# Slot attentions: one ring of six PSUM banks, four heads of turned scores at once, and the softmax maximum in two halves

## The chip, the cores and the metric

The kernel runs on one core of one Trainium2 chip. The metric is device time in microseconds (us) for one execution of the whole program. The program is a 16-layer hybrid network, so a time is a sum over layers that run one after another with a barrier between them.

## What is computed

The input is x of 8 sequences with 256 tokens each and width 128. The layers around the change are multi-head attentions with 16 heads of 8 dimensions. Cut to what matters, each of them computes, for a sequence:

```
q, k, v = h @ Wq (+ bq), h @ Wk (+ bk), h @ Wv (+ bv)      # 16 heads of 8
s = q @ k.T * scale                                        # 256 x 256 a head; causal or windowed in two layers
p = softmax(s)
o = p @ v
```

`L0_attn_b` is causal, `L2_attn_b` has no mask, `L3_attn_b` has a causal window of 64, and the encoder layer `L3_ffn` (it comes twice, as layers 13 and 15) runs, for each of the 8 sequences, the two experts that a gate picked; each is an unmasked attention, a layer norm, a two-layer network of 512 hidden units and another layer norm. All of it is float32.

## The kernel before

Four kinds of stage share the code of the change: three calls of `slot_attention_stage` (8 units, one for each sequence) and two of `encoder_stage` (16 units, sequence times expert). A unit is cut into `NC` = 4 chunks of `HP` = 4 heads, and each head sits in a slot of 32 partitions. One step of the stage's loop (`for u in a.steps`) works on a chunk. So a slot attention has 32 chunk steps and an encoder 64.

A chunk's work runs over several engines:

- **scores** (`slot_scores_pe`, L628): TensorE multiplies queries with keys, four heads in four row strips of the array at once, into `S`, four PSUM banks, one a head. Masked stages add the mask by eight more products (L647). VectorE takes the negative row maximum from `S` (`slot_max_dve`, L756).
- **turned maximum** (`slot_turn_max_pe`, L688): TensorE turns the maxima into `X`, the one bank that all side work shares; VectorE adds them to the queries (`slot_add_max_dve`, L771) and so makes `qA`.
- **turned scores** (`slot_turned_scores_pe`, L652): keys times `qA`, that is the score already less its maximum, with keys on the partitions. Two heads at a time, p = 0 and p = 1, into `E`, two banks. ScalarE takes the exponential of each pair of heads into `sT` (`slot_exp_act`, L725).
- **PV** (`slot_pv_pe`, L670): the exponentials times v into `OB`; ScalarE copies (`slot_out_act`, L732), TensorE turns the copy (`slot_turn_out_pe`, L698), and VectorE divides by the sum (`slot_norm_dve`, L779).

There is no scheduler: each engine executes its instructions in the order in which its block writes them, and waits at semaphores. Between the chunk's operations stand the **items**: projections of q and k (`qk`) and of v (`v`), the turn of the normed input (`h`), and for the encoder the turn of the attention's output (`t`), its projection (`y`), the turn of the first norm's output (`t1`), and the two-layer network (`f1`, `f2`, `f3`). Each step has at most one early and one late item, from the tables at the head of the stage. In the encoder every step has both: early `qk`, `f1`, `y`, `f3`, late `t1`, `t`, `f2`, `v` for the chunks 0 to 3. A slot attention has `qk` and `v` early in chunks 0 and 1 and `h` late in chunk 3; the windowed one also has `y` early in 3 and `t` late in 2.

Every item is a product into bank `X`, then a copy out of it: by VectorE for `y` and `f3`, by ScalarE for all others. The bank is handed on in the fixed order early item, late item, turned maximum. TensorE waits before each (`slot_x_pe`) until the one before it has been copied out:

```
n = a.number[item]
if n:
    pe.wait_ge(b.sems.x_used, n)
```

Of the kernel before, what the change touches and what calls it, by code (L numbers as in the profile page):

```python
# [384 lines left out]
class SlotPlan:  # L385
# [34 lines left out]
    def at(self, kt):  # L420

        return slice(kt * self.n[0], kt * self.n[0] + self.n[kt])

# [86 lines left out]
class SlotBuffers:  # L510


    def __init__(self, st, a):
# [5 lines left out]
        self.sT = st.sb("sT", [P, 2, a.HP, TT * a.n[0]])  # L519
# [4 lines left out]
        self.S = st.ps("S", [P, a.HP, 512])  # L524
        self.E = st.ps("E", [P, 2, 512])
# [102 lines left out]
def slot_scores_pe(pe, g, a, b, u):  # L628
# [4 lines left out]
    if u:  # L633
        pe.wait_ge(s.maxed, u)
    for t in range(TT):
        lo, hi = a.keys[t]
        for h in range(a.HP):
            rows = slice(32 * h, 32 * (h + 1))
            last = pe.matmul(b.S[:, h, t * T:t * T + hi - lo], b.qk[rows, r % 2, 0, c, t * P:(t + 1) * P],  # L639
                             b.qk[rows, r % 2, 1, c, lo:hi], start=(t == 0), stop=(a.mask is None and t == TT - 1),  # L640
                             skip_group_check=True, tile_position=(32 * h, 0))
    if a.mask is not None:
        for h in range(a.HP):
            for t in range(TT):
                lo, hi = a.masked[t]
                at = t * T + lo - a.keys[t][0]
                last = pe.matmul(b.S[:, h, at:at + hi - lo], g.ident_bf[:], g.masks[a.mask][:, t, lo:hi],  # L647
                                 start=False, stop=(t == TT - 1), skip_group_check=True)
    last.then_inc(s.scored, 1)


def slot_turned_scores_pe(pe, a, b, u, p):  # L652
# [3 lines left out]
    if p == 0:  # L656
        pe.wait_ge(s.x_used, a.number[("m", u)] + 1)
    if 2 * u + p:
        pe.wait_ge(s.expd, 2 * u + p)
    for kt in range(TT):  # L660
        lo, hi = a.queries[kt]
        for i in range(2):
            rows = slice(32 * (2 * p + i), 32 * (2 * p + i + 1))
            last = pe.matmul(b.E[:, i, a.at(kt)], b.qk[rows, r % 2, 1, c, kt * P:(kt + 1) * P],  # L664
                             b.qA[rows, u % 2, lo:hi], start=True, stop=True, skip_group_check=True,
                             tile_position=(32 * (2 * p + i), 0))
    last.then_inc(s.st_mm, 1)


def slot_pv_pe(pe, a, b, j):  # L670
# [8 lines left out]
    for kt in range(TT):  # L679
        lo, hi = a.queries[kt]  # L680
        for h in range(a.HP):
            last = pe.matmul(b.OB[32 * h:32 * (h + 1), lo:hi], b.v[:, r % 2, kt, a.HP * c + h, :],  # L682
                             b.sT[:, j % 2, h, a.at(kt)], start=(kt == 0), stop=(kt == TT - 1),
# [4 lines left out]
def slot_turn_max_pe(pe, g, a, b, u):  # L688
# [3 lines left out]
    pe.wait_ge(s.maxed, u + 1)  # L692
# [32 lines left out]
def slot_exp_act(act, a, b, u, p):  # L725
# [3 lines left out]
    act.activation(b.sT[:, u % 2, 2 * p:2 * p + 2, 0:a.width], b.E[:, :, 0:a.width], ACT.Exp).then_inc(s.expd, 1)  # L729
# [8 lines left out]
def slot_cut_pool(pool, a, b, u):  # L738

    s = b.sems  # L740
    for p in range(2):
        pool.wait_ge(s.expd, 2 * u + p + 1)
        m = b.sT[:, u % 2, 2 * p:2 * p + 2, :].rearrange("p h (k q) -> p (h k) q", k=TT)
# [12 lines left out]
def slot_max_dve(dve, a, b, u):  # L756

    s = b.sems
    dve.wait_ge(s.scored, u + 1)
    if a.mask is None:  # L760
        ins = dve.tensor_reduce(b.negm[:, u % 2, :, a.HD::32].rearrange("p t h -> p h t"),  # L761
                                b.S[:].rearrange("p h (t k) -> p h t k", t=TT), AX_X, ALU.max, negate=True)
    else:
        for t in range(TT):
            lo, hi = a.keys[t]
            ins = dve.tensor_reduce(b.negm[:, u % 2, t, a.HD::32], b.S[:, :, t * T:t * T + hi - lo], AX_X, ALU.max,  # L766
# [26 lines left out]
def slot_attention_stage(nc, g, name, W, scale, mask=None, project=False):  # L793
# [7 lines left out]
    with Stage(nc, name) as st:  # L801
# [9 lines left out]
        with nc.Block() as block:  # L811
# [6 lines left out]
            def _(pool):  # L818
# [3 lines left out]
                for u in range(U + 1):  # L822
# [4 lines left out]
                    if not project and (r := a.ends(u - 1)) is not None:  # L827
                        xb = g.x[:, TT * r:TT * r + TT, :]
                        pool.wait_ge(s.o_norm, u)
# [5 lines left out]
            def _(pe):  # L835
# [14 lines left out]
                for u in a.steps:  # L850
                    if u + 1 < U:
                        slot_scores_pe(pe, g, a, b, u + 1)
                    for item in a.early(u):
                        other(item)
                    if 0 <= u < U:
                        slot_turned_scores_pe(pe, a, b, u, 0)
                    for item in a.late(u):
                        other(item)
                    if 0 <= u - 1 < U:
                        slot_pv_pe(pe, a, b, u - 1)  # L860
                    if 0 <= u < U:
                        slot_turned_scores_pe(pe, a, b, u, 1)
# [2481 lines left out]
```

## Time and profile before

| | us |
|---|---|
| median of 3 runs | 3464.14 |
| lowest and highest run | 3460.72 to 3464.31 |
| the profiled execution's own time | 3461.5 |
| its span | 3459.8 |
| scores of the causal attention, first to last | 698.4 to 857.0 |
| of the unmasked attention | 1638.7 to 1812.9 |
| of the first encoder | 2332.7 to 2746.3 |
| of the windowed attention | 2801.4 to 2953.6 |
| of the second encoder | 2996.3 to 3411.9 |

The profile shows for each instruction when it started and how long it took; where an engine was idle before it, it names what released it. A float32 product of the code appears in the profile as two matmuls, so the eight products of scores appear as x16. A chunk step is read from one start of the scores (L639) to the next, and a unit is four such steps. PE is TensorE's matmuls, PEld its weight loads, ACT ScalarE, DVE VectorE, POOL GpSimd. PEclk is the granted TensorE clock: 1.00 is 2.4 GHz, 0.50 is 1.2 GHz.

### The profile page before, as it was taken

The page shows a single profiled execution, that of the slowest core. Times are in us where ns is not written, and L with a number is a line of the kernel's source. Part 1 is how long each engine was busy: PE and PEld are TensorE (multiplying, and loading weights), DVE is VectorE, ACT ScalarE, POOL GpSimd, SP SyncE. Part 2 cuts the span into 40 slices and gives each one's busy share as a digit, 9 for nine tenths or more (in the row PEclk, how much of TensorE's full clock was granted, in tenths as well). Part 3 has the DMA queues.
Part 4 walks back from the last instruction along what each step waited for, and adds up shares of the span by engine and source line. Part 5 has one row for each costly group of instructions (what it writes and reads, how often), then busy time and mean ns, then how long its engine had stood idle before and what let it go on. Part 6 is the DMA issues. An engine that isn't in the chain of part 4 may idle for free. (4 is left out here: it accounts for less than half of the span.)

```text
span 3459.8 us, 60788 instructions
## 1 busy us (share of the span) xinstructions
PE 3006.9 (87%) x23920; PEld 2002.9 (58%) x23920; DVE 1991.5 (58%) x4069; ACT 1409.0 (41%) x2886; POOL 959.6 (28%) x1321
## 2 busy tenths in 40 slices
PE   5689699999699879776996699979999979799997
PEld 1234377766477646455665466756666657466665
DVE  5998655445655568642563466655556545455564
ACT  4344244434344324212452244434554434245543
POOL 1455333223223110122003433330222245212222
PEclk7799799999799969777897799988999989699998
DMA  1000100010000000010100000002222101112221
GB/s 75 1 1 0 50 1 1 1 29 20 1 1 1 1 1 2 1 65 19 27 20 21 7 1 1 1 7 62 67 65 70 50 21 27 51 38 67 65 70 42
DMA packets 46937, 90.94 MB, mean 26 GB/s; under 512 B 6052, under 2 KB 34524, under 8 KB 45888
## 3 DMA queue, kind: packets, MB, share of 16 engines
q1 hardware_dynamic: 44608, 86.43, 8.2%
q8 instruction: 194, 3.18, 0.4%
q0 software_dynamic: 2048, 0.61, 0.1%
q14 instruction: 87, 0.71, 0.1%
HBM read 70.16 MB, written 19.14 MB: 26 GB/s over the span
## 5 line engine op out<-in xcount | busy, mean ns | idle before, releaser
L729 ACT ACTIVATE s_sT<-s_E 128x1024 f32<-128x1024 f32 (+2 forms) x448 | 424.6, 948 | 487.0 <-PE s_E L664 486.2
L664 PE MATMUL s_E<-s_qA,s_qk 32*128 32x256 f32 (+2 forms) x3584 | 484.3, 388 | 15.1 <-ACT s_sT L729 6.1
L664 PEld LDWEIGHTS s_E<-s_qA,s_qk 32*128 32x128 f32 x3584 | 313.0, 189 | 164.8 <-ACT s_sT L729 76.4
L761 DVE TENSOR_REDUCE s_negm<-s_S 128x8 f32<-128x2048 f32 x160 | 366.9, 2293 | 69.8 <-PE s_S L639 61.6
L776 DVE TENSOR_TENSOR s_qA<-s_qk,s_X 128x256 f32<-128x256 f32 x224 | 94.4, 421 | 415.3 <-PE s_X L694 415.3
L639 PE MATMUL s_S<-s_qk 32*128 32x256 f32 (+2 forms) x3584 | 255.9, 402 | 15.1 <-DMA s_qk<-s_pk 15.1
L682 PE MATMUL s_OB<-s_sT,s_v 128*32 128x256 f32 (+2 forms) x3584 | 227.7, 372 | 4.9 <-POOL s_sT L751 1.9
L2470 POOL TENSOR_TENSOR all_hT<-s0s_hs,s0s_cb 128x1024 f32<-128x1024 f32 x64 | 150.5, 2352 | 197.0 <-DVE s0s_hs L2504 179.8
L639 PEld LDWEIGHTS s_S<-s_qk 32*128 32x128 f32 x3584 | 158.8, 195 | 59.9 <-issue 54.8
L1352 POOL TENSOR_TENSOR s_pr<-s_pr,s_rinv 128x1024 f32<-128x1024 f32 x64 | 121.1, 1893 | 225.2 <-DVE s_rinv L1458 225.2
L1430 ACT ACTIVATE s_pr<-s_S,s_negmax 128x256 f32<-128x256 f32 x256 | 118.5, 470 | 135.4 <-DVE s_negmax L1461 135.4
L1040 POOL TENSOR_TENSOR s_veps<-s_mv,all_eps 128x2 f32<-128x2 f32 x64 | 16.6, 260 | 538.1 <-DVE s_mv L1245 538.1
L2504 DVE TENSOR_TENSOR_SCAN s0s_hs<-s0s_dA,s0s_dBu 128x1024 f32<-128x1024 f32 x64 | 145.7, 2281 | 0.0
L682 PEld LDWEIGHTS s_OB<-s_sT,s_v 128*32 128x32 f32 x3584 | 94.6, 110 | 88.0 <-issue 38.7
L766 DVE TENSOR_REDUCE s_negm<-s_S 128x4 f32<-128x512 f32 (+2 forms) x128 | 108.2, 888 | 55.7 <-PE s_S L647 55.7
L2443 PE MATMUL s0s_Y<-all_hT,all_ident 128*128 128x512 f32 x256 | 129.6, 631 | 9.0 <-DVE s0s_yv L2515 6.4
L744 POOL TENSOR_SCALAR_AFFINE_SELECT s_sT<-s_sT 128x512 f32<-128x512 f32 x128 | 81.2, 634 | 195.4 <-ACT s_sT L729 195.4
L694 PE MATMUL s_X<-all_ident,s_negm 128*128 128x128 f32 x448 | 101.2, 309 | 12.5 <-DVE s_negm L761 8.8
L2408 PE MATMUL s0s_BB<-s0s_xparts,all_ident_bf 80*128 80x512 bf16 x192 | 57.9, 414 | 57.5 <-DVE s0s_xparts L2487 41.5
L1461 DVE TENSOR_REDUCE s_negmax<-s_S 128x4 f32<-128x1024 f32 x64 | 78.3, 1223 | 37.5 <-PE s_S L1370 37.5
L735 ACT ACTIVATE s_oc<-s_OB 128x256 f32<-128x256 f32 x224 | 85.9, 383 | 33.0 <-PE s_OB L682 28.2
L2461 ACT ACTIVATE s0s_cb<-s0s_CB 128x512 f32<-128x512 f32 x64 | 38.2, 597 | 138.3 <-PE s0s_CB L2408 137.1
(571 smaller groups left out, 6263.6 us busy)
## 6 DMA issues: line engine op xcount, KB each, us to landing
s_wB<-enc_b SPq DMA_DIRECT2D x32, 962.5 KB, 4.9
s_scratch<-s_pk SPq DMA_DIRECT2D x51, 256.0 KB, 2.0
s_qk<-s_scratch SPq DMA_DIRECT2D x204, 64.0 KB
s_wA<-enc_a SPq DMA_DIRECT2D x32, 193.0 KB, 4.2
big<-moe SPq DMA_DIRECT2D x2, 2347.0 KB, 12.4
big<-routed SPq DMA_DIRECT2D x2, 2084.0 KB
all_W<-weights SPq DMA_DIRECT2D x1, 2296.0 KB, 16.1
all_W<-weights SPq DMA_DIRECT2D x1, 2295.5 KB, 11.1
```

The costliest lines, as they stand in the source:

```text
L639: last = pe.matmul(b.S[:, h, t * T:t * T + hi - lo], b.qk[rows, r % 2, 0, c, t * P:(t + 1) * P], b.qk[rows, r % 2, 1, c, lo:hi], start=(t ...
L664: last = pe.matmul(b.E[:, i, a.at(kt)], b.qk[rows, r % 2, 1, c, kt * P:(kt + 1) * P], b.qA[rows, u % 2, lo:hi], start=True, stop=True, ski ...
L682: last = pe.matmul(b.OB[32 * h:32 * (h + 1), lo:hi], b.v[:, r % 2, kt, a.HP * c + h, :], b.sT[:, j % 2, h, a.at(kt)], start=(kt == 0), sto ...
L694: last = pe.transpose(b.X[:, t * P:(t + 1) * P], b.negm[:, u % 2, t, :], g.ident[:])
L729: act.activation(b.sT[:, u % 2, 2 * p:2 * p + 2, 0:a.width], b.E[:, :, 0:a.width], ACT.Exp).then_inc(s.expd, 1)
L761: ins = dve.tensor_reduce(b.negm[:, u % 2, :, a.HD::32].rearrange("p t h -> p h t"), b.S[:].rearrange("p h (t k) -> p h t k", t=TT), AX_X, ...
L766: ins = dve.tensor_reduce(b.negm[:, u % 2, t, a.HD::32], b.S[:, :, t * T:t * T + hi - lo], AX_X, ALU.max, negate=True)
L1352: pool.tensor_tensor(p, p, rinv[:, u % 3, :, :].rearrange("p h t -> p (h t)").unsqueeze(2) .to_broadcast([P, 2 * TT, T]), ALU.mult).then_i ...
L1430: ins = act.activation(pr[:, u % 3, h, t, :], S[:, u % 2, h, t * T:(t + 1) * T], ACT.Exp, bias=negmax[:, u % 3, h, t:t + 1], accum_out=sum ...
L2443: last = pe.matmul(Y[:, m, :], g.ident[:], hc[:, j % 2, m, :], start=first, stop=last_)
L2470: pool.tensor_tensor(hc[:, q % 2, :, :], hs[:, q % 2, :, :], cb[:, q % 2, :].unsqueeze(1).to_broadcast([P, M, C]), ALU.mult)\
L2504: dve.tensor_tensor_scan(out=hs[:, q % 2, :, :].rearrange("p m c -> p (m c)"), data0=dA[:, q % 2, :, :].rearrange("p m c -> p (m c)"), dat ...
```

## The change

- `S` and `E` become one ring `R` of six banks, used as three pairs. The scores of chunk u take pairs 4u-2 and 4u-1, its turned scores pairs 4u+4 and 4u+5, all modulo 3. Turned scores of chunk u therefore use, as their second pair, the pair that held the first half of the scores of chunk u+1.
- Turned scores run all four heads at once instead of two times two. They wait for the exponentials of the chunk before, and for the first half of the maximum of the next chunk.
- Each chunk's maximum is two reductions over two heads each.
- PV moves on TensorE from between the two turned scores to right behind the scores. In the two masked stages PV, its copy and the division come two steps behind instead of one (`lag`), with three buffers of `sT`.
- On ScalarE the copy of PV's result moves to the head of the step, and both exponentials stand together, ahead of the late item.
- On TensorE the turn of the output moves ahead of the late item, and the turn of the maximum to the end.
- On VectorE the maximum moves ahead of the early item, the addition of the turned maximum behind the division; in the encoder the first norm's last operation moves from the head of its step to behind the addition.

```diff
@@ class SlotPlan
         self.units, self.U, self.mask = units, units * self.NC, mask
+        self.lag = 1 if mask is None else 2
...
+    def pair(self, first, p):
+
+        n = 2 * ((first + p) % 3)
+        return slice(n, n + 2)
+
+    def scores_at(self, u, p):
+
+        return self.pair(4 * u - 2, p)
+
+    def turned_at(self, u, p):
+
+        return self.pair(4 * u + 4, p)
@@ class SlotBuffers
-        self.sT = st.sb("sT", [P, 2, a.HP, TT * a.n[0]])
+        self.sT = st.sb("sT", [P, a.lag + 1, a.HP, TT * a.n[0]])
...
-        self.S = st.ps("S", [P, a.HP, 512])
-        self.E = st.ps("E", [P, 2, 512])
+        self.R = st.ps("R", [P, 6, 512])
@@ def slot_scores_pe(pe, g, a, b, u):
     if u:
-        pe.wait_ge(s.maxed, u)
+        pe.wait_ge(s.maxed, 2 * u)
+    if u >= 2:
+        pe.wait_ge(s.expd, 2 * u - 3)
+    S = [b.R[:, a.scores_at(u, h // 2), :][:, h % 2, :] for h in range(a.HP)]
...
+            if a.mask is None and t == TT - 1 and h % 2:
+                last.then_inc(s.scored, 1)
@@
+def slot_turned_scores_pe(pe, a, b, u):
...
+    pe.wait_ge(s.x_used, a.number[("m", u)] + 1)
+    if u:
+        pe.wait_ge(s.expd, 2 * u)
+    if u + 1 < a.U:
+        pe.wait_ge(s.maxed, 2 * (u + 1) + 1)
     for kt in range(TT):
         lo, hi = a.queries[kt]
-        for i in range(2):
...
+        for h in range(a.HP):
+            rows = slice(32 * h, 32 * (h + 1))
+            last = pe.matmul(b.R[:, a.turned_at(u, h // 2), :][:, h % 2, a.at(kt)],
+                             b.qk[rows, r % 2, 1, c, kt * P:(kt + 1) * P], b.qA[rows, u % 2, lo:hi], start=True,
+                             stop=True, skip_group_check=True, tile_position=(32 * h, 0))
+            if kt == TT - 1 and h % 2:
+                last.then_inc(s.st_mm, 1)
@@ def slot_turn_max_pe(pe, g, a, b, u):
     slot_x_pe(pe, a, b, ("m", u))
-    pe.wait_ge(s.maxed, u + 1)
+    pe.wait_ge(s.maxed, 2 * (u + 1))
@@
-def slot_max_dve(dve, a, b, u):
+def slot_max_dve(dve, a, b, u, p):
...
-    dve.wait_ge(s.scored, u + 1)
+    dve.wait_ge(s.scored, 2 * u + p + 1)
@@ both stages, TensorE's loop
                 for u in a.steps:
                     if u + 1 < U:
                         slot_scores_pe(pe, g, a, b, u + 1)
+                    if 0 <= u - a.lag < U:
+                        slot_pv_pe(pe, a, b, u - a.lag)
                     for item in a.early(u):
                         other(item)
                     if 0 <= u < U:
-                        slot_turned_scores_pe(pe, a, b, u, 0)
+                        slot_turned_scores_pe(pe, a, b, u)
+                    if 0 <= u - a.lag < U:
+                        slot_turn_out_pe(pe, g, a, b, u - a.lag)
                     for item in a.late(u):
                         other(item)
-                    if 0 <= u - 1 < U:
-                        slot_pv_pe(pe, a, b, u - 1)
-                    if 0 <= u < U:
-                        slot_turned_scores_pe(pe, a, b, u, 1)
                     if u + 1 < U:
                         slot_turn_max_pe(pe, g, a, b, u + 1)
-                    if 0 <= u - 1 < U:
-                        slot_turn_out_pe(pe, g, a, b, u - 1)
@@ both stages, ScalarE's loop
                 for u in a.steps:
+                    if 0 <= u - a.lag < U:
+                        slot_out_act(act, a, b, u - a.lag)
                     for item in a.early(u):
                         other(item)
                     if 0 <= u < U:
                         slot_exp_act(act, a, b, u, 0)
+                        slot_exp_act(act, a, b, u, 1)
                     for item in a.late(u):
                         other(item)
-                    if 0 <= u - 1 < U:
-                        slot_out_act(act, a, b, u - 1)
-                    if 0 <= u < U:
-                        slot_exp_act(act, a, b, u, 1)
@@ both stages, VectorE's loop
                 for u in a.steps:
+                    if u + 1 < U:
+                        for p in range(2):
+                            slot_max_dve(dve, a, b, u + 1, p)
                     for item in a.early(u):
...
-                    if u + 1 < U:
-                        slot_max_dve(dve, a, b, u + 1)
-                        slot_add_max_dve(dve, a, b, u + 1)
...
                         slot_norm_dve(dve, a, b, j)
+                    if u + 1 < U:
+                        slot_add_max_dve(dve, a, b, u + 1)
```

How the order moves, first on TensorE in an encoder, from the scores of a step with the early item `qk` and the late item `t1` to the scores of the next. Before (`s_S` and `s_E` are the scores and turned scores, `s_OB` from `s_sT` is PV and from `s_oc` the turn of the output, `s_X` from `s_negm` the turn of the maximum):

```order
L639 MATMUL s_S<-s_qk 128x256 x8
L600 MATMUL s_X<-all_hT,s_wA 128x256
L601 MATMUL s_X<-all_hT,s_wA 128x256
L664 MATMUL s_E<-s_qA,s_qk 128x256 x4
L1095 MATMUL s_X<-all_ident,s_x 128x128 x2
L682 MATMUL s_OB<-s_sT,s_v 32x256 x8
L664 MATMUL s_E<-s_qA,s_qk 128x256 x4
L694 MATMUL s_X<-all_ident,s_negm 128x128 x2
L703 MATMUL s_OB<-all_ident,s_oc 128x128 x2
```

And with the change (`s_R` from `s_qk` alone is the scores, from `s_qA` the turned scores):

```order
L655 MATMUL s_R<-s_qk 128x256 x8
L703 MATMUL s_OB<-s_sT,s_v 32x256 x8
L613 MATMUL s_X<-all_hT,s_wA 128x256
L614 MATMUL s_X<-all_hT,s_wA 128x256
L684 MATMUL s_R<-s_qA,s_qk 128x256 x8
L724 MATMUL s_OB<-all_ident,s_oc 128x128 x2
L1118 MATMUL s_X<-all_ident,s_x 128x128 x2
L715 MATMUL s_X<-all_ident,s_negm 128x128 x2
```

The two turned scores of four products are one of eight, PV stands right behind the scores, and the turn of the maximum closes the step, behind the late item (L1118).

On ScalarE in an encoder, the same step from its first exponential (`s_sT`) to the next step's early item. Before:

```order
L729 ACTIVATE s_sT<-s_E 128x1024
L1160 ACTIVATE s_x1T<-s_X 128x256
L735 ACTIVATE s_oc<-s_OB 128x256
L729 ACTIVATE s_sT<-s_E 128x1024
L1164 ACTIVATE s_hid<-s_X,s_wB 128x256 x2
L729 ACTIVATE s_sT<-s_E 128x1024
```

And with the change:

```order
L750 ACTIVATE s_sT<-s_R 128x1024 x2
L1181 ACTIVATE s_x1T<-s_X 128x256
L757 ACTIVATE s_oc<-s_OB 128x256
L1185 ACTIVATE s_hid<-s_X,s_wB 128x256 x2
L750 ACTIVATE s_sT<-s_R 128x1024 x2
```

The copy of the late item (`s_x1T`) stood between the two exponentials and now stands behind both; the copy of PV's result (`s_oc`) moved into the next step.

## Rows read from the trace of the kernel before

**Rows 1.** Busy time, share of the span and instructions of each engine.
```profile
PE 3006.9 (87%) x23920; PEld 2002.9 (58%) x23920; DVE 1991.5 (58%) x4069; ACT 1409.0 (41%) x2886; POOL 959.6 (28%) x1321
```

**Rows 2.** The chain of waits that ended last, by line.
```profile
PE s_E L664 4%; PE s_S L639 2%; PE s_OB L682 2%; PE s_X L1099 1%; PE s_X L1104 1%; PE s_X L694 1%; PE s_OB L703 0%; PE s_X L600 0%; PE s_X L721 0%; PE s_X L604 0%; PE s_X L601 0%; PE s_X L713 0%; PE s_X L1095 0%; ACT s_sT L729 0%; DVE s_negm L761 0%
```

**Rows 3.** Windows: stretch, its us, busy per engine, clock, DMA share, GB/s.
```profile
3130.33:3156.66 26.33, 26.33 (x249) 17.02 (x249) 15.69 (x33) 13.24 (x22) 5.92 (x10) 1.00 0.21 63
1766.06:1787.45 21.39, 21.02 (x221) 13.28 (x220) 13.27 (x23) 11.21 (x17) 2.26 (x4) 1.00 0.10 26
760.99:781.35 20.36, 19.99 (x252) 14.07 (x251) 11.65 (x27) 9.51 (x17) 7.39 (x12) 1.00 0.10 27
2871.10:2890.78 19.68, 19.44 (x258) 14.62 (x257) 11.04 (x28) 8.76 (x18) 11.22 (x27) 1.00 0.11 28
```

**Rows 4.** Timeline, second encoder: start us, us, engine, line, operation, idle before.
```profile
3130.26 2.05 PE L1104 MATMUL s_X<-s_wB,s_hid 128*128 128x128 f32 x16
...
3132.24 1.13 PE L664 MATMUL s_E<-s_qA,s_qk 32*128 32x256 f32 x8
...
3133.30 0.71 PE L604 MATMUL s_X<-s_wA,all_hT 128*128 128x128 f32 x4
...
3133.94 1.07 PE L682 MATMUL s_OB<-s_sT,s_v 128*32 128x256 f32 x16
...
3134.94 1.13 PE L664 MATMUL s_E<-s_qA,s_qk 32*128 32x256 f32 x8
...
3136.01 0.44 PE L694 MATMUL s_X<-all_ident,s_negm 128*128 128x128 f32 x2
...
3136.28 0.38 PE L703 MATMUL s_OB<-all_ident,s_oc 128*128 128x128 f32 x2
...
3136.59 1.15 PE L639 MATMUL s_S<-s_qk 32*128 32x256 f32 x16
...
3137.67 0.70 PE L600 MATMUL s_X<-all_hT,s_wA 128*128 128x256 f32 x2
3137.80 2.29 DVE L761 TENSOR_REDUCE s_negm<-s_S 128x8 f32<-128x2048 f32 x1 [0.53 <-PE s_S L639]
...
3138.73 1.13 PE L664 MATMUL s_E<-s_qA,s_qk 32*128 32x256 f32 x8
...
3139.91 1.02 ACT L729 ACTIVATE s_sT<-s_E 128x1024 f32<-128x1024 f32 x1 [0.18 <-PE s_E L664]
...
3140.83 0.38 ACT L1160 ACTIVATE s_x1T<-s_X 128x256 f32<-128x256 f32 x1
...
3147.05 0.47 ACT L1158 ACTIVATE s_oT<-s_X,s_wB 128x256 f32<-128x256 f32 x1
...
3152.98 0.84 ACT L1164 ACTIVATE s_hid<-s_X,s_wB 128x256 f32<-128x256 f32 x2
```

**Rows 5.** Costliest groups, whole program: a maximum over half the size.
```profile
L1461 DVE TENSOR_REDUCE s_negmax<-s_S 128x4 f32<-128x1024 f32 x64 | 78.3, 1223 | 37.5 <-PE s_S L1370 37.5
```

**Rows 6.** Timeline, unmasked attention: an exponential, and the turned scores behind it.
```profile
1741.94 1.02 ACT L729 ACTIVATE s_sT<-s_E 128x1024 f32<-128x1024 f32 x1 [0.23 <-PE s_E L664]
...
1743.02 0.73 PEld L664 LDWEIGHTS s_E<-s_qA,s_qk 32*128 32x128 f32 x8 [0.60 <-ACT s_sT L729]
1743.02 1.13 PE L664 MATMUL s_E<-s_qA,s_qk 32*128 32x256 f32 x8
```

**Rows 7.** Chain of waits, second encoder's start: start us, us, what.
```profile
3011.45 2.02 PE s_S L639 x16
3013.47 1.69 PE s_E L664 x8
...
3020.08 1.15 PE s_S L639 x5
```

**Rows 8.** Windows of two other stages, columns as in rows 3.
```profile
1400.00:1500.00 100.00, 77.00 (x337) 52.93 (x329) 43.08 (x146) 26.11 (x42) 15.02 (x20) 0.72 0.00 1
1850.00:1900.00 50.00, 38.69 (x203) 29.49 (x202) 14.30 (x41) 13.46 (x29) 17.55 (x16) 0.86 0.08 23
```

More of the change, by code:

```diff
@@ L682, in slot_pv_pe @@
             last = pe.matmul(b.OB[32 * h:32 * (h + 1), lo:hi], b.v[:, r % 2, kt, a.HP * c + h, :],
-                             b.sT[:, j % 2, h, a.at(kt)], start=(kt == 0), stop=(kt == TT - 1),
+                             b.sT[:, j % (a.lag + 1), h, a.at(kt)], start=(kt == 0), stop=(kt == TT - 1),
                              skip_group_check=True, tile_position=(0, 32 * h))
@@ L821, in _ @@
                 slot_setup_pool(pool, a, b)
-                for u in range(U + 1):
+                for u in range(U + a.lag):
                     if u < U and mask is not None:
@@ L826, in _ @@
                         ln.power_pool(pool, g, r)
-                    if not project and (r := a.ends(u - 1)) is not None:
+                    if not project and (r := a.ends(u - a.lag)) is not None:
                         xb = g.x[:, TT * r:TT * r + TT, :]
-                        pool.wait_ge(s.o_norm, u)
+                        pool.wait_ge(s.o_norm, u - a.lag + 1)
                         pool.tensor_tensor(xb, xb, b.o[:, r % 2, :, :], ALU.add).then_inc(s.o_taken, 1)
@@ L914, in _ @@
                                .then_inc(s.x_used, 1)
[L915 to L918 removed]
+                    j = u - a.lag
                     if 0 <= j < U:
@@ L1116, in _ @@
                     pe.wait_ge(pick_rows_done, k + 1)
-                    pe.matmul(b.E[0:1, k, 0:B], g.ones[0:B, 0:1], pick_rows[:, :, k], start=True, stop=True)\
+                    pe.matmul(b.R[0:1, 4 + k, 0:B], g.ones[0:B, 0:1], pick_rows[:, :, k], start=True, stop=True)\
                       .then_inc(picks_mm, 1)
@@ L1127, in _ @@
                         slot_scores_pe(pe, g, a, b, u + 1)
+                    if 0 <= u - a.lag < U:
+                        slot_pv_pe(pe, a, b, u - a.lag)
                     for item in a.early(u):
@@ L1177, in _ @@
                 for u in a.steps:
+                    if 0 <= u - a.lag < U:
+                        slot_out_act(act, a, b, u - a.lag)
                     for item in a.early(u):
@@ L1249, in _ @@
                 for u in a.steps:
[L1250 to L1258 removed]
+                    if u + 1 < U:
+                        for p in range(2):
+                            slot_max_dve(dve, a, b, u + 1, p)
                     for item in a.early(u):
@@ L1276, in _ @@
                             dve.sem_inc(s.x_used, 1)
+                    if 0 <= u - a.lag < U:
+                        slot_norm_dve(dve, a, b, u - a.lag)
                     if u + 1 < U:
-                        slot_max_dve(dve, a, b, u + 1)
                         slot_add_max_dve(dve, a, b, u + 1)
-                    if 0 <= u - 1 < U:
-                        slot_norm_dve(dve, a, b, u - 1)
+                    if (r := at_step(u, 3, -1)) is not None:
+                        dve.wait_ge(rstd_ready, powers)
+                        if r:
+                            dve.wait_ge(x1b_ready, r)
+                            dve.wait_ge(s.x_mm, a.number[("t1", r - 1)] + 1)
+                        for t in range(TT):
+                            ins = dve.tensor_scalar(x1[:, t, :], r1[:, t, :], mv[:, 0, t, 0:1], rstd[:, 0, t:t + 1],
+                                                    ALU.subtract, ALU.mult)
+                        ins.then_inc(x1_norm, 1)
                     if (r := at_step(u, 2, -1)) is not None:
```

61 lines of the change are left out of this document (19 added, 42 removed).

## The prediction

> **What bounds the kernel now.** I read the page first, then the chain of waits, then windows, then the timeline. The page has TensorE's matmuls busy in 87% of the span and ScalarE in 41% [rows 1]. The chain that ended last is TensorE's nearly throughout, its turned scores first (4%), then scores and PV [rows 2]. The windows each hold one unit of four chunk steps, in this order: an encoder, the unmasked, the causal and the windowed attention [rows 3]. The encoder's unit takes 26.33 us, and TensorE is busy in all of it; the others are within 0.4 us of that. So TensorE binds there, and I must see what a step is made of. The timeline gives the time from the start of each group of matmuls to the next [rows 4]: scores to `qk` 1.08 (3136.59 to 3137.67), `qk` to turned scores 1.06, first turned scores to `v` 1.06, `v` to PV 0.64, PV to second turned scores 1.00, these to the turned maximum 1.07, that to the turned output 0.27, that to scores 0.31. The scores are 16 matmuls in 1.08 us, each half of the turned scores is 8 in 1.06 or 1.07. Four heads cost no more than two.
>
> **What the change removes.** All four heads of turned scores in one group should cost what scores cost, so one group of 1.07 us goes from every step. There are 64 steps in each encoder and 32 in each of three attentions. TensorE's work in an encoder unit becomes 26.33 - 4 x 1.07 = 22.05 us. If only TensorE bound, two encoders (32 units) would give 32 x 4.28 = 137 us, and the attentions at most 96 x 1.07 = 103 us. The question is what is late next.
>
> **What it adds, the encoder.** Bank `X` goes early item, late item, turned maximum, and the turned maximum waits until the late item is copied out. All four late items of an encoder unit are ScalarE's to copy. Before, that copy stood between the two exponentials, and PV and the second turned scores covered it; the copy of `t1` started at 3140.83, and TensorE never waited [rows 4]. Now it stands behind both exponentials, which themselves begin only when the one group of turned scores is through, and all that TensorE has in the meantime is the turned output and the late item. Behind the waiting turned maximum are queued the next scores, PV and the next early item, so the ring closes. From turned scores to turned scores:
>
> - to the first exponential 1.18 (3138.73 to 3139.91), each exponential to the next copy 0.92 (3139.91 to 3140.83), twice 1.84 [rows 4];
> - the late copy: `t1` 0.38, `t` 0.47, `f2` 0.84, `v` like `t1` 0.38, together 2.07 a unit [rows 4];
> - ScalarE's end to TensorE's start 0.06 (1741.94 + 1.02 to 1743.02) [rows 6];
> - turned maximum to scores 0.27, scores to PV 1.08, PV to the early item 1.00; the early item `qk` 1.06, `f1` (the same four matmuls) 1.06, `y` (as `v`) 0.64, `f3` 1.98 (3130.26 to 3132.24), together 4.74 a unit [rows 4].
>
> The fixed part is 1.18 + 1.84 + 0.06 + 0.27 + 1.08 + 1.00 = 5.43 a step, 21.72 a unit. With 2.07 and 4.74 the unit takes **28.5 us** against 26.33. TensorE then idles some 1.4 to 1.8 us in each step. Cost: 32 x 2.2 = **+70 us**. The halved maximum costs 2 x 1.22 [rows 5] against 2.29 [rows 4], and its first half is there 1.21 + 1.22 + 0.06 = 2.49 us after the scores start, earlier than scores, PV and any early item are through (2.72 at least), so it costs nothing here. The x1 operation that moved behind the addition on VectorE has a whole step until `t1` needs it: nothing.
>
> **The unmasked attention.** A step without an item now goes scores to turned scores 2.49 (the first half of the maximum is the cover that is missing), to the end of the first exponential 1.18 + 1.02, and 0.06 to the next scores, which wait for it because they reuse its banks: 4.75. With `v` it is 2.72 + 2.26 = 4.98, with `qk` 3.14 + 2.26 = 5.40, with the late `h` 2.49 + 1.18 + 1.84 + 0.38 + 0.06 + 0.27 = 6.22. Together 21.35 against 21.39 [rows 3]: **0 us**. The gain is eaten by latencies.
>
> **The masked attentions.** The same ring with shorter exponentials and maxima. GpSimd's cut of the exponentials has a step more by the lag. I take -3 us for both; the ends are 16 units x 4.28 = -68 us, should TensorE alone bind, and +10 us.
>
> **Starts.** Each of the five stages starts with the clock at 0.50, where a step took 8.6 us (3011.45 to 3020.08) and was TensorE's alone, with groups twice as long [rows 7]. One group of 2 us fewer against the same waits on ScalarE: I take -1 us for some ten such steps, **-10 us**; ends -20 and +10.
>
> **The clock.** An encoder unit would have TensorE busy in 22.05 of 28.5 us, 77%. The kernel has two long stretches with just that share (77.00 of 100, 38.69 of 50), and the granted clock there was 0.72 and 0.86 [rows 8], against 1.00 in all four steady units, which are 98% busy or more [rows 3]. The part of the ring that is TensorE's is 4 x (1.18 + 0.27 + 1.08 + 1.00) + 4.74 = 18.9 us a unit. At a mean clock of 0.86 it grows by 18.9 x (1/0.86 - 1) = 3.1 us, 98 us over 32 units; at 1.00 by nothing. Gaps here are short and evenly spread, so I take a third of that way, a clock of 0.95: 18.9 x 0.053 x 32 = **+32 us**. The Trainium skill ("TensorE: Matmul & The Clock Gate", on HAM oscillation) says that gaps between bursts of matmuls can throttle the engine again and again; by gaps as short as these it would expect no fall, and the sum would end 32 us lower.
>
> **The sum.** 3461.5 (the profiled execution's own time) + 70 + 0 - 3 - 10 + 32 = 3550.5. The median of the runs, 3464.14, stands 0.1% above the profiled one; I leave that out and say **3550 us**. A difference under 0.2%, 7 us, can't be told from no change.
>
> **Rivals.**
>
> *TensorE gets its time back.* If the late copy does not hold the turned maximum (because ScalarE is only half busy), the stage stays TensorE's and the sum is 3461.5 - 137 - 103 = 3222 at the most, 3325 if only the encoders gain. For it: ScalarE is busy in 13.24 of 26.33 us [rows 3]. Against: it is the order, not the load, that holds it, and nothing in the code lets the copy pass the exponentials. The point from which it decides is the late copy's end: TensorE is through turned scores, turned output and a short late item some 1.65 us after the turned scores start (1.07 + 0.31 + 0.27 for groups like these before [rows 4]), and the copy ends 1.18 + 1.84 + 0.38 = 3.4 us after it. "TensorEngine Tiling (Array Packing)" of the Trainium skill, on the PSUM bottleneck, says that tiling speeds TensorE but not the emptying of PSUM. By throughput that would bind only from 22.05 us a unit, far above ScalarE's 13.24; the trace agrees that load is not the limit. Chance 0.09, and 0.03 that gain and loss cancel.
>
> *No clock dips.* Then 3518. Chance 0.30.
>
> *The clock settles at 0.50 in the encoders.* Then each group takes twice its time [rows 7]: the ring grows by 18.9 us a unit, 600 us in all. It decides once the half-speed step, too, has gaps. Half-speed groups fill most of the gaps, which speaks against: 0.04.
>
> *Four heads aren't faster than two.* Turned scores would take 2.1 us: 1.07 x 128 + 1.07 x 96 at most on the ring, +137 to +240 us, 3655 to 3760. Against it: the scores already do it in four banks at 1.08 us. Chance 0.03.
>
> My forecast with some dips has the remaining 0.51. The range 3495 to 3630 takes in the case without dips less the lower end of the starts and part of the masked ones (3518 - 10 - 13), and the case of 0.86 (3518 + 98) with the starts' upper end. Faster 0.09, same 0.03, slower 0.88.
>
> **What would show it.** Right: an encoder unit of 28 to 31 us, the turned maximum's weight load waiting for ScalarE's late copy 1.4 to 1.8 us in every encoder step; one group of 16 turned scores with 1.06 us to the next; in the unmasked attention a wait of turned scores for VectorE's maximum in steps without an item, and of scores for the first exponential; the granted clock below 1.00 in places in the encoders. Wrong: TensorE without idle time in the encoders; a turned-score group of 2 us; an encoder unit under 26.3 us.

## The result, and the profile after

The changed kernel takes 3573.43 us (median of 4 runs, 3568.79 to 3578.36) against 3462.43 us for the kernel before in the same session. The ratio is 1.032 (95% interval 1.030 to 1.034): **slower**, by 111 us. The forecast was 3550, range 3495 to 3630. The profiled execution's span is 3575.1 us against 3459.8.

The page of the changed kernel, in the views of [rows 1] and [rows 2] (busy time; the chain by line) and the group of instructions that turns the maximum:

```profile
PE 2842.3 (80%) x23920; PEld 1873.6 (52%) x23920; DVE 2019.2 (56%) x4357; ACT 1382.7 (39%) x2886; POOL 961.6 (27%) x1321
...
ACT s_sT L750 3%; PE s_R L655 2%; PE s_OB L703 2%; PE s_R L684 2%; PE s_X L1127 1%; PE s_X L715 1%; PE s_X L1122 1%; ACT s_hid L1185 0%; PE s_X L742 0%; PE s_X L613 0%; DMA s_scratch<-s_pk 0%; PE s_X L614 0%; ACT s_oT L1179 0%; DVE s_negm L785 0%; ACT s_x1T L1181 0%
...
L715 PE MATMUL s_X<-all_ident,s_negm 128*128 128x128 f32 x448 | 95.2, 295 | 231.3 <-ACT s_oT L1179 54.1
```

TensorE has 165 us less busy time and the program takes 115 us more. The chain no longer runs on TensorE alone: the exponentials (L750) now lead it. And TensorE was idle 231 us before the turned maxima (L715), where the kernel before had 12.5:

```profile
L694 PE MATMUL s_X<-all_ident,s_negm 128*128 128x128 f32 x448 | 101.2, 309 | 12.5 <-DVE s_negm L761 8.8
```

Where the time went, by stage, measured from the first scores to the last:

| stage | before | after | unit before | unit after |
|---|---|---|---|---|
| causal | 158.1 | 153.5 | 20.36 | 20.00 |
| unmasked | 173.5 | 172.6 | 21.39 | 21.78, half of them 23.4 |
| first encoder | 412.9 | 466.0 | 26.34 | 28.86, most 30.44 |
| windowed | 151.7 | 151.1 | 19.67 | 20.06 |
| second encoder | 414.8 | 465.7 | 26.34 | 28.86, most 30.44 |

(A unit is four steps, scores to scores; where two numbers stand, the first is a unit at full clock throughout and the second is what most units, or half of them, took. The mean in the encoders is 30.33.) The two encoders lose 104 us and the three attentions gain 6. The other 17 of the span's 115 us lie outside these stretches.

The timeline of the changed kernel in the second encoder, one step with the late item `f2`, columns as in [rows 4]:

```profile
3223.50 1.15 PE L684 MATMUL s_R<-s_qA,s_qk 32*128 32x256 f32 x16
...
3224.57 0.44 PE L724 MATMUL s_OB<-all_ident,s_oc 128*128 128x128 f32 x2
3224.68 1.94 ACT L750 ACTIVATE s_sT<-s_R 128x1024 f32<-128x1024 f32 x2 [1.30 <-PE s_R L684]
...
3224.85 1.04 PE L1122 MATMUL s_X<-s_x1T,s_wB 128*128 128x256 f32 x4
...
3226.50 0.84 ACT L1185 ACTIVATE s_hid<-s_X,s_wB 128x256 f32<-128x256 f32 x2
...
3227.40 0.44 PE L715 MATMUL s_X<-all_ident,s_negm 128*128 128x128 f32 x2 [1.51 <-ACT s_hid L1185]
...
3227.77 1.15 PE L655 MATMUL s_R<-s_qk 32*128 32x256 f32 x16
...
3228.84 1.07 PE L703 MATMUL s_OB<-s_sT,s_v 128*32 128x256 f32 x16
...
3229.84 2.05 PE L1127 MATMUL s_X<-s_wB,s_hid 128*128 128x128 f32 x16
...
3231.82 1.15 PE L684 MATMUL s_R<-s_qA,s_qk 32*128 32x256 f32 x16
```

This is the ring that was forecast. All four heads of turned scores do run in 1.07 us (3223.50 to 3224.57). The exponentials start 1.18 behind them, the late copy 1.82 later at 3226.50, and only when it has ended, at 3227.34, can TensorE turn the maximum (3227.40). Scores, PV, the early item and the next turned scores are queued behind that. TensorE had nothing to do for 1.51 us.

Windows of the changed kernel, columns as in [rows 3]: 300 us of an encoder, then within it a stretch at half speed and one at full speed:

```profile
3100.00:3400.00 300.00, 235.13 (x2463) 147.25 (x2461) 159.08 (x341) 126.83 (x219) 55.29 (x94) 0.95 0.17 52
```
```profile
3151.20:3154.60 3.40, 3.40 (x33) 1.80 (x32) 2.35 (x7) 0.00 (x0) 1.60 (x3) 0.52 0.30 68
3154.60:3181.90 27.30, 20.79 (x228) 13.44 (x224) 13.85 (x30) 12.71 (x22) 4.51 (x7) 1.00 0.16 56
```

The kernel before held 1.00 here with TensorE always busy [rows 3]. Now TensorE is busy 78% of the time, and the clock falls to 1.2 GHz again and again; in the half-speed stretch it is busy throughout, since its groups take twice as long.

### The profile page after: what moved, and what is told of

Same layout as the page of the kernel before. It is cut to its first block and busy times, and to the rows that moved or that the text cites. A ratio compares the mean times of both kernels' runs of the same rounds, so it can differ in the third digit from the quotient of the medians.

```text
span 3575.1 us, 61234 instructions
## 1 busy us (share of the span) xinstructions
PE 2842.3 (80%) x23920; PEld 1873.6 (52%) x23920; DVE 2019.2 (56%) x4357; ACT 1382.7 (39%) x2886; POOL 961.6 (27%) x1321
## 5 line engine op out<-in xcount | busy, mean ns | idle before, releaser
L750 ACT ACTIVATE s_sT<-s_R 128x1024 f32<-128x1024 f32 (+2 forms) x448 | 400.0, 945 | 201.6 <-PE s_R L684 200.8
L785 DVE TENSOR_REDUCE s_negm<-s_R 128x4 f32<-128x1024 f32 x320 | 376.9, 1220 | 94.9 <-PE s_R L655 86.6
L655 PE MATMUL s_R<-s_qk 32*128 32x256 f32 (+2 forms) x3584 | 260.3, 407 | 63.0 <-ACT s_sT L750 35.9
L715 PE MATMUL s_X<-all_ident,s_negm 128*128 128x128 f32 x448 | 95.2, 295 | 231.3 <-ACT s_oT L1179 54.1
L684 PE MATMUL s_R<-s_qA,s_qk 32*128 32x256 f32 (+2 forms) x3584 | 243.0, 385 | 16.1 <-DVE s_negm L785 10.7
L703 PE MATMUL s_OB<-s_sT,s_v 128*32 128x256 f32 (+2 forms) x3584 | 246.7, 397 | 9.7 <-ACT s_sT L750 6.4
L655 PEld LDWEIGHTS s_R<-s_qk 32*128 32x128 f32 x3584 | 163.0, 196 | 109.0 <-issue 91.7
L684 PEld LDWEIGHTS s_R<-s_qA,s_qk 32*128 32x128 f32 x3584 | 164.2, 187 | 80.1 <-issue 66.1
L715 PEld LDWEIGHTS s_X<-all_ident,s_negm 128*128 128x128 f32 x448 | 48.9, 142 | 272.3 <-ACT s_oT L1179 61.2
L809 DVE RECIPROCAL s_rden<-s_OB 128x8 f32<-128x8 f32 x224 | 46.5, 208 | 234.6 <-PE s_OB L724 234.6
L790 DVE TENSOR_REDUCE s_negm<-s_R 128x2 f32<-128x256 f32 (+2 forms) x256 | 116.3, 518 | 59.7 <-PE s_R L665 59.6
```

Of the source, the lines that this page charges most:

```text
L655: last = pe.matmul(S[h][:, t * T:t * T + hi - lo], b.qk[rows, r % 2, 0, c, t * P:(t + 1) * P], b.qk[rows, r % 2, 1, c, lo:hi], start=(t == ...
L684: last = pe.matmul(b.R[:, a.turned_at(u, h // 2), :][:, h % 2, a.at(kt)], b.qk[rows, r % 2, 1, c, kt * P:(kt + 1) * P], b.qA[rows, u % 2, ...
L715: last = pe.transpose(b.X[:, t * P:(t + 1) * P], b.negm[:, u % 2, t, :], g.ident[:])
L750: act.activation(b.sT[:, u % (a.lag + 1), 2 * p:2 * p + 2, 0:a.width], b.R[:, a.turned_at(u, p), 0:a.width], ACT.Exp).then_inc(s.expd, 1)
L785: ins = dve.tensor_reduce(b.negm[:, u % 2, :, at].rearrange("p t h -> p h t"), S.rearrange("p h (t k) -> p h t k", t=TT), AX_X, ALU.max, n ...
L790: ins = dve.tensor_reduce(b.negm[:, u % 2, t, at], S[:, :, t * T:t * T + hi - lo], AX_X, ALU.max, negate=True)
```

## The experiments

All ratios are against the kernel before, measured on the same chip in the same session. Differences to the change, or from one experiment to another, are of medians from different sessions; the kernel before took 3461.93 to 3465.37 us in these. "Unit" is an encoder's, from one scores' start to the fourth after it, in the steady part.

**e1: the copy between the exponentials again.** ScalarE's loop, both stages:

```diff
                         slot_exp_act(act, a, b, u, 0)
-                        slot_exp_act(act, a, b, u, 1)
                     for item in a.late(u):
                         other(item)
+                    if 0 <= u < U:
+                        slot_exp_act(act, a, b, u, 1)
```

> The changed kernel with one edit: on ScalarE the late item's copy stands between the two exponentials again, as before the change. Theory (the late copy behind both exponentials holds the turned maximum and closes a ring of 28.9 us a unit in the encoders): the ring loses one exponential, 0.92 us, a step where the late item is early enough, the unit goes to about 25.8 us, granted clock near 1.00 in the encoders, the program to about 3414 us, faster than before the change. Rival (the time is lost to the clock or to the ring of banks, not to the copy's place): the unit stays at 28 us or more and the program at 3540 to 3573.

Measured 3418.54 us, ratio 0.989 (0.986 to 0.991): 155 us under the change and 43 us under the kernel before. Every steady unit takes 25.53 us at full clock. The loss is this one place in ScalarE's order; the rest of the change together is a gain.

**e2: the maximum is turned before the late item.** The order of bank `X`, TensorE's loop and VectorE's:

```diff
-            order += self.early(u) + self.late(u)
+            order += self.early(u)
             if u + 1 < self.U:
                 order.append(("m", u + 1))
+            order += self.late(u)
@@ TensorE, both stages
                         slot_turned_scores_pe(pe, a, b, u)
+                    if u + 1 < U:
+                        slot_turn_max_pe(pe, g, a, b, u + 1)
                     if 0 <= u - a.lag < U:
                         slot_turn_out_pe(pe, g, a, b, u - a.lag)
                     for item in a.late(u):
                         other(item)
-                    if u + 1 < U:
-                        slot_turn_max_pe(pe, g, a, b, u + 1)
@@ VectorE, both stages: slot_add_max_dve ahead of slot_norm_dve
```

> The changed kernel with bank X handed on as early item, turned maximum, late item: the turned maximum stands on TensorE right behind the turned scores, the addition on VectorE ahead of the division, and the late item last in the step. Theory: the late copy is then needed only by the next step's early item, 2 us after the next scores start, so it is off the ring; what is left is turned scores 1.07, maximum's turn to the addition's end 0.95, late item, scores, PV, early item: about 24.3 us a unit in the encoders and 3358 us in all. Rival (the exponentials themselves are the ring, through the banks): no better than with the copy between the exponentials, 3410 or more.

Measured 3364.46 us, ratio 0.971 (0.969 to 0.974): the best version, 98 us under the kernel before and 209 under the change. A unit is 23.79 us, at full clock. The timeline of e2 shows what takes the ring's place:

```profile
3223.55 1.15 PE L685 MATMUL s_R<-s_qA,s_qk 32*128 32x256 f32 x16
...
3224.63 0.44 PE L716 MATMUL s_X<-all_ident,s_negm 128*128 128x128 f32 x2
3224.73 1.94 ACT L751 ACTIVATE s_sT<-s_R 128x1024 f32<-128x1024 f32 x2 [2.64 <-PE s_R L685]
...
3225.10 0.42 DVE L801 TENSOR_TENSOR s_qA<-s_qk,s_X 128x256 f32<-128x256 f32 x1 [0.92 <-PE s_X L716]
...
3225.58 0.60 PE L618 MATMUL s_X<-s_wA,all_hT 128*128 128x128 f32 x3 [0.29 <-DVE s_qA L801]
```

The maximum is turned 1.08 us behind the turned scores, without a wait; the late item waits 0.3 us for VectorE's addition, and its copy is nobody's concern until the next early item.

**e3: the turned scores wait for the whole maximum.**

```diff
-        pe.wait_ge(s.maxed, 2 * (u + 1) + 1)
+        pe.wait_ge(s.maxed, 2 * (u + 1) + 2)
```

> The changed kernel, but the turned scores wait for both halves of the next chunk's maximum instead of the first. Theory (first half is off the ring in the encoders but on it in steps without an item): the turned scores start 3.63 us after the scores instead of 3.15, 3.15, 2.72 and 4.06, so +1.9 us a unit in the encoders (+60 us) and about +2.5 to +3.7 us a unit in the attentions (+65), 3700 us in all. Rival (VectorE is never late, the ring has slack): within 10 us of the change, 3573.

Measured 3688.81 us, ratio 1.065 (1.063 to 1.068), 115 us over the change. A full-clock encoder unit is 30.88 (28.86 + 2.0, forecast +1.9); the attentions' units are at full clock 1.5 us (windowed), 2.5 us (causal) and 3.7 us (unmasked) longer. So the second half of the reduction is hidden only because the wait is on the first, and that wait is worth 115 us. A maximum in one reduction, 2.29 us [rows 4] against two of 1.22, was not run in this order.

**e4: two heads at a time, side by side.** The loop over pairs of heads is outside again, with one signal behind each pair, and nothing stands between the two groups:

```diff
-    for kt in range(TT):
-        lo, hi = a.queries[kt]
-        for h in range(a.HP):
+    for p in range(2):
+        for kt in range(TT):
+            lo, hi = a.queries[kt]
+            for h in range(2 * p, 2 * p + 2):
...
+        last.then_inc(s.st_mm, 1)
```

> The changed kernel with turned scores again two heads at a time (two groups of 1.06 us back to back, each pair signalled by its own group), all else as changed. Theory (what TensorE saves by four heads is idle time in this order): the second exponential is ready 2.2 us after the first group starts, when ScalarE comes to it anyway; the encoders stay at 28.9 to 29.3 us a unit and the clock rises, since TensorE has 1.07 us more to do in each gap; attentions lose some 0.4 us in steps without an item. 3560 to 3590 us in all, though TensorE does 224 x 1.07 = 240 us more. Rival (TensorE's work still counts): 3700 to 3813.

Measured 3567.73 us, ratio 1.031 (1.029 to 1.033), 6 us under the change; the runs of the two overlap (3567.36 to 3580.31 here). The time is as expected, but not for the reason given: the work didn't grow. The timeline of e4 has both groups as one:

```profile
3226.81 1.16 PE L685 MATMUL s_R<-s_qA,s_qk 32*128 32x256 f32 x16
```

Sixteen matmuls in 1.16 us, in two-head order as in four-head order (1.15). Both orders put the matmuls of the four row strips next to each other; in the kernel before other work stood between the two pairs, and each took 1.06 (e6 shows the same in the changed kernel). So e4 tells nothing about the price of four heads, and e6 and e7 were made for that.

**e5: the gap filled.** Two needless products in each step with a late item, into a pair of the ring that is free there:

```diff
+    pe.wait_ge(s.maxed, 2 * (u + 1))
+    if u >= 1 and a.late(u - 1):
+        for k in range(2):
+            pe.matmul(b.R[:, a.scores_at(u, 1), :][:, k % 2, 0:T], g.ident[:], b.qk[:, (u // a.NC) % 2, 1, u % a.NC, :],
+                      start=True, stop=True, skip_group_check=True)
     slot_x_pe(pe, a, b, ("m", u))
-    pe.wait_ge(s.maxed, 2 * (u + 1))
```

> The changed kernel with two needless float32 products (128x128 by 128x256, some 0.53 us each) on TensorE in every step that has a late item, written into a free pair of the ring just before the wait for the late copy, so that they fill most of its 1.5 to 1.8 us of idle time; nothing reads them. Theory (half-speed stretches in the encoders come from these idle times and cost 30.3 - 28.9 = 1.5 us a unit): the granted clock stays at 1.00 in the encoders' steady part, every unit takes 28.9 us, and doing more work makes the program some 50 us faster than the change, about 3515 us. Rival (the clock's stretches are hidden or don't come from the gaps): 3573 or more.

Measured 3535.06 us, ratio 1.021 (1.017 to 1.024): 38 us faster than the change, with more work (forecast some 50). The window of 300 us, as above:

```profile
3100.00:3400.00 300.00, 267.92 (x2740) 177.25 (x2743) 165.73 (x360) 133.29 (x230) 59.21 (x100) 1.00 0.19 59
```

TensorE is busy 89% of the time, the clock is 1.00, and every steady encoder unit takes 28.86 us, the length of the change's own undisturbed units. That prices the clock apart from the ring. From first to last scores the encoders are 17.4 and 18.0 us shorter than in the change, and the unmasked attention 5.0 us (all its steady units take 21.78); the masked ones are the same within 0.4. Together 40 us, as the program's 38.

**e6: two groups that can't overlap.** As e4, but with the turn of the output between the pairs:

```diff
+                        slot_turned_scores_pe(pe, a, b, u, 0)
                     if 0 <= u - a.lag < U:
                         slot_turn_out_pe(pe, g, a, b, u - a.lag)
+                    if 0 <= u < U:
+                        slot_turned_scores_pe(pe, a, b, u, 1)
```

> The changed kernel with the turned scores in two groups of two heads that can't overlap: the turn of the output stands between them. (With the groups side by side they ran in 1.16 us all the same.) TensorE has 224 x 1.07 = 240 us more to do. Theory (what four heads at once save is spent waiting in this order): the second exponential starts 2.56 us behind the first group's start instead of 2.10, +0.46 us a step, 30.7 us a unit in the encoders with fewer half-speed stretches; attentions +0.5 us a step; about 3630 us. Rival (TensorE's work counts in full): 3800 us.

Measured 3690.54 us, ratio 1.067 (1.064 to 1.069). 117 us over the change: less than half of the 240 us that TensorE has to do more, but twice the forecast. The two groups are apart, each 1.06 us to what follows it:

```profile
3384.00 1.13 PE L685 MATMUL s_R<-s_qA,s_qk 32*128 32x256 f32 x8
...
3385.06 0.44 PE L724 MATMUL s_OB<-all_ident,s_oc 128*128 128x128 f32 x2
...
3385.43 1.13 PE L685 MATMUL s_R<-s_qA,s_qk 32*128 32x256 f32 x8
```

The ring's part was nearly right, 31.06 us in an encoder unit at full clock (forecast 30.7) and some 2.1 us more in the attentions' (forecast 2); that alone is some 100 of the 117 us. The fewer half-speed stretches that were to give part of it back did not come: TensorE is busier,

```profile
3200.00:3500.00 300.00, 264.41 (x2306) 161.70 (x2298) 148.46 (x318) 122.91 (x205) 53.45 (x91) 0.95 0.17 51
```

88% of the time against 78%, and still at 0.95, so the mean unit is 32.3. e5 has 89% and 1.00. The busy share alone doesn't tell whether the clock falls. The masked attentions, which had no half-speed stretches behind their start in the change, got them too (causal units of 22.08 at full clock and up to 25.0).

**e7: the same on top of e2,** with the turn of the maximum between the pairs.

> The kernel with the maximum turned first (e2), and the turned scores in two groups of two heads with the turn of the maximum between them. Theory (with the late copy off the ring TensorE binds again, so that here four heads at once is worth most of its 1.07 us a step; part of it, 0.35 us, fills a wait for the addition): +0.7 us a step in the encoders, 26.6 us a unit, attentions +0.5 us a step; about 3500 us. Rival (the order alone brought the gain of e2, four heads nothing): 3365 to 3380 us.

Measured 3494.84 us, ratio 1.009 (1.006 to 1.012), with 26.45 us a unit. Where the late copy is off the ring, four heads at once is worth 3494.84 - 3364.46 = 130 us. In the change, splitting the heads cost 117 us, nearly as much: either order hides about half of the 240 us of TensorE work.

**e8: the kernel before with only the copy moved.**

```diff
                         slot_exp_act(act, a, b, u, 0)
-                    for item in a.late(u):
-                        other(item)
                     if 0 <= u - 1 < U:
                         slot_out_act(act, a, b, u - 1)
                     if 0 <= u < U:
                         slot_exp_act(act, a, b, u, 1)
+                    for item in a.late(u):
+                        other(item)
```

> The kernel before with one part of the change alone: on ScalarE the late item's copy stands behind both exponentials. Theory: the turned maximum, which came 1.07 us behind the second turned scores' start, now waits 1.18 + 0.92 + copy + 0.06 behind it, so 4 x 1.09 + 2.07 = 6.4 us more a unit in the encoders (32.8 us), some +2 us in each unit of the attentions with one late item, and more with a lower clock: about 3700 us. Rival (the copy's place costs nothing by itself, it is the new TensorE order that loses): 3462 us.

Measured 3828.53 us, ratio 1.107 (1.104 to 1.110): 364 us for one moved copy, more than the 240 expected. A unit takes 37.55 us, not 32.8. The timeline of e8, at full speed, has the wait that was reckoned, 3421.84 - 3420.49 + 1.17 = 2.5 us from the second turned scores to the turned maximum:

```profile
3420.49 1.02 ACT L729 ACTIVATE s_sT<-s_E 128x1024 f32<-128x1024 f32 x1 [0.66 <-PE s_E L664]
3421.41 0.38 ACT L1160 ACTIVATE s_x1T<-s_X 128x256 f32<-128x256 f32 x1
...
3421.84 0.44 PE L694 MATMUL s_X<-all_ident,s_negm 128*128 128x128 f32 x2 [1.40 <-ACT s_x1T L1160]
```

and its window of one unit shows the rest of it:

```profile
3378.85:3416.40 37.55, 31.41 (x249) 20.30 (x248) 15.61 (x32) 13.15 (x22) 5.94 (x10) 0.86 0.15 46
```

The clock is 0.86. As an estimate, with the unit's 26.34 us of TensorE work [rows 3] all on the ring, a clock of 0.86 adds 26.34 x (1/0.86 - 1) = 4.3 us to 32.8, 37.1 of the 37.55. So e8 prices the copy's place together with the clock that it cost; e1 is the cleaner measure of the place alone.

**e9: the lag of the masked stages back at one.**

```diff
-        self.lag = 1 if mask is None else 2
+        self.lag = 1
```

> The changed kernel with the lag of PV in the two masked stages back at one step (two buffers of exponentials). Theory (the lag is what hides GpSimd's cut): the causal stage's two cuts end just as PV comes, within 0.5 us a unit; the windowed stage's, 1.34 us each, end some 1.2 us behind it in three of four steps, so about +3.5 us a unit there; +28 us in all, about 3600 us. Rival (the cut was hidden anyway): 3573.

Measured 3598.65 us, ratio 1.039 (1.037 to 1.042), 25 us over the change (forecast 28). The windowed stage's unit goes from 20.06 to 22.61 us, the causal one's stays at 20.0: the second step of lag hides GpSimd's cut in the windowed stage and is not needed in the causal one.

**e10: PV behind the late item again,** in the unmasked stages.

```diff
-                    if 0 <= u - a.lag < U:
-                        slot_pv_pe(pe, a, b, u - a.lag)
+                    if a.lag == 2 and 0 <= u - 2 < U:
+                        slot_pv_pe(pe, a, b, u - 2)
+                    if a.lag == 1 and 0 <= u - 2 < U:
+                        slot_turn_out_pe(pe, g, a, b, u - 2)
...
                     for item in a.late(u):
                         other(item)
+                    if a.lag == 1 and 0 <= u - 1 < U:
+                        slot_pv_pe(pe, a, b, u - 1)
```

> The changed kernel with one part undone in the unmasked stages: PV stands behind the late item again instead of right behind the scores, its copy behind the late copy and the turn of its result behind the next scores; all else as changed. Theory (PV ahead of the turned scores lengthens the ring by 1 us a step while TensorE idles where PV used to be): turned scores to the next scores 3.45 us plus the late copy, scores to turned scores 2.49 or, with f3, 3.37: 26.7 us a unit in the encoders with hardly any half-speed stretches, the unmasked attention as before, about 3455 us. Rival (PV's place is neutral, the copy alone decides): 28.9 us a unit or more, 3540 to 3573.

Measured 3478.82 us, ratio 1.003 (1.002 to 1.005): 95 us under the change. A unit takes 26.66 us at a clock of 1.00, as forecast to 0.1 us. The program is still 24 us over the forecast 3455: the encoders' first three units stayed as long as in the change (79.8 against 80.8 us in the first encoder), so the two encoders gained 93 us and not 116. The unmasked attention's unit is 22.6 us, 0.9 longer than its undisturbed 21.78, where "as before" was forecast. In the timeline of e10 PV takes most of the wait, 0.66 us being left:

```profile
3201.05 1.07 PE L703 MATMUL s_OB<-s_sT,s_v 128*32 128x256 f32 x16
3202.33 0.39 ACT L637 ACTIVATE s_v<-s_X 128x256 f32<-128x256 f32 x1
...
3202.78 0.44 PE L715 MATMUL s_X<-all_ident,s_negm 128*128 128x128 f32 x2 [0.66 <-ACT s_v L637]
```

So there are three ways to mend the ring, and they are worth different amounts: move the copy (155 us), fill the wait with PV (95 us), or take the copy out of the ring (209 us).

## Why the prediction was right

**Four heads in the time of two** was right: 16 matmuls in 1.07 us. e4 adds that the loop order has no part in it, only that nothing stands between.

**The encoder's ring**, 28.5 us a unit and +70 us, was right in mechanism and some 0.3 us short in size: the full-clock unit is 28.86. The term "turned maximum to scores 0.27" was taken from the step before, where another turn followed it [rows 4]; with scores behind it, it takes 0.37 (3227.40 to 3227.77). Over the four steps of a unit that is the 0.3 to 0.4 us, over 32 units some 11 us, which the encoders' faster first units gave back: with the clock at 1.00 (e5) they are 69 us longer than before, where 70 was forecast. e1, e2 and e8 show that the copy's place is the cause, e10 that PV's place made the wait bare.

**The clock** was the term least well founded, +32 us by a guessed 0.95. The windows give just 0.95, and e5 prices it at 38 us for the program. That the guess came out is luck in part, for the way to the number was loose: e6 at 88% busy has the same 0.95 as the change at 78%, so a busy share like that of [rows 8] was not enough to fix the clock. The Trainium skill's "TensorE: Matmul & The Clock Gate", on HAM oscillation, was read in the prediction as expecting no fall from gaps this short; the trace shows falls with no single idle time over 1.81 us in the encoders' steady parts, and the measurement decides. That reading was of one section only: the page's next, "A second HAM failure mode: psum-queue depth-cycling", tells of a kernel whose short idle times between groups of matmuls, being frequent, were enough, and the trace agrees with that.

**The unmasked attention**, forecast at 21.35 a unit and unchanged, has 21.78 at full clock and 23.4 in half of its steady units: the same 0.1 us a step, and half-speed stretches that the sum had only for the encoders. Its faster start (11.3 us at half speed behind the first scores against 27.1) gave that back, and the stage as a whole is 0.9 us shorter. The waits that were named for it are there (timeline of the changed kernel, a step without an item, then one with `qk`):

```profile
1756.92 1.15 PE L684 MATMUL s_R<-s_qA,s_qk 32*128 32x256 f32 x16 [0.40 <-DVE s_negm L785]
...
1763.87 1.15 PE L684 MATMUL s_R<-s_qA,s_qk 32*128 32x256 f32 x16
1765.04 1.94 ACT L750 ACTIVATE s_sT<-s_R 128x1024 f32<-128x1024 f32 x2 [0.23 <-PE s_R L684]
...
1766.21 1.15 PE L655 MATMUL s_R<-s_qk 32*128 32x256 f32 x16 [0.61 <-ACT s_sT L750]
```

The turned scores wait 0.40 us for VectorE's maximum, and the scores 0.61 us for the first exponential, whose banks they take: 1766.21 is 2.34 behind the turned scores, where 2.26 was reckoned.

**The masked attentions and the starts**, -3 and -10 us, came to -5 us from first to last scores in the masked stages, their faster starts among it. The starts alone gave more than was forecast: the first units of the five stages take 116 us together, against 136 before.

**What the sum left out.** Everything that it priced, the five stretches from first to last scores, came to +98 us, where 89 was forecast. The other 17 us lie outside them, and the sum had no term for that. Of these, some 5 us lie behind the last scores of each encoder, up to the next stage's first scores or the end. In e10, with PV back behind the late item, these tails are as before within 1.3 us, so PV's new place, with what moved along with it, makes them longer. Some 5 us more lie between the last scores of the causal attention and the first of the unmasked one, and 2 ahead of the causal one; the first of these stretches, some 780 us and most of it other layers, varies from 773 to 789 us over the experiments, so no cause is shown for that part.

**The rival that TensorE gets its time back** fell, in the change. e2 shows what it needed: with the late copy out of the ring TensorE's saving is paid out, 98 us faster than before.

## What to carry to other kernels

Where each engine runs its instructions in the order written, ask of every copy that frees a shared buffer what stands ahead of it in its own queue, not how busy that engine is: ScalarE was half idle (13.24 of 26.33 us a unit [rows 3]), and one copy placed behind two exponentials turned a gain of 1.1% (e1) into a loss of 3.2%. Work taken from the engine that binds pays only if nothing on its ring waits longer than before; walk the ring once, term by term, from the rows, and where it closes through another engine, put either the bound engine's own work into that wait or the waited-for step ahead of it. Saved TensorE time that turns into idle time can cost twice, since the clock may fall in the steps around it.

## What the runs showed of the hardware

- Float32 matmuls of different 32-row strips overlap where they stand next to each other: eight products in pair order took 1.16 us (e4) and in four-head order 1.15 (the change), but 2 x 1.06 with other work between the pairs (e6, [rows 4]).
- More work can be faster: two useless products a step (e5) took the granted clock in the encoders from 0.95 to 1.00 and 38 us off the program.
- The mean busy share doesn't predict the clock. The change at 78% and e6 at 88% were both granted 0.95, e8 at 84% 0.86, e10 at 84% (26.66 us a unit, below) and e5 at 89% 1.00.

```profile
3050.00:3350.00 300.00, 252.19 (x2794) 160.97 (x2788) 175.45 (x382) 138.34 (x247) 61.13 (x104) 1.00 0.20 59
```

That is e10's window. At half speed TensorE looks busier than its work is, but that doesn't explain the order: within a stretch that was at full clock throughout, e6 was busy 87% of the time, and its clock fell again behind it.

```profile
3352.20:3505.70 153.50, 134.30 (x1216) 83.84 (x1216) 78.16 (x172) 66.26 (x110) 28.34 (x48) 1.00 0.18 57
```

How the idle time is spread may matter; which pattern makes the clock fall is left open.
